# Four instructions of a 16-step turn moved by one step, and two PSUM banks exchanged

## The chip, the cores and the metric

One core of a Trainium2 chip. The metric is the device time of one execution in microseconds (us). A difference is worth telling from 0.2% on, which is 7 us here.

## What is computed

The input is normalised, `xn = (x - mean) / sqrt(var + 1e-5)`, for 16 sequences of 256 tokens with 128 channels. Two branches read it: a state-space branch `s` (short convolutions, a selective scan over 256 positions with 16 states) and a transformer of 6 layers, whose output goes through `silu` to give `g`. The result is `x + s * g`. The change lies in the transformer:

```python
def attn_layer(x, Wqkv, qs, ksc, Wo):
    q, k, v = jnp.split(x @ Wqkv, 3, -1)          # 16 heads of 64
    q = l2norm(q) * qs
    k = l2norm(k) * ksc
    q = q * cos * scale + rotate_half(q) * sin * scale
    k = k * cos * inv + rotate_half(k) * sin * inv
    out = local_attention(q, k, v)                # windows of 32, softmax
    return out @ Wo

def ffn_layer(x, g, bln, W1, b1, W2, b2):
    mu = x.mean(-1, keepdims=True)
    var = ((x - mu) ** 2).mean(-1, keepdims=True)
    xn = (x - mu) / jnp.sqrt(var + 1e-05) * g + bln
    a, gate = jnp.split(xn @ W1 + b1, 2, -1)
    return a * jax.nn.gelu(gate, approximate=False) @ W2 + b2

for i in range(6):
    x = attn_layer(shift_tokens(x), ...) + x
    x = ffn_layer(shift_tokens(x), ...) + x
```

## The kernel before

The tokens are cut into 8 groups of 512 (two sequences). The state-space branch comes first; its core time ends a little after 300 us. Then 6 layers of 8 groups, 48 items, pass through a software pipeline of **turns**. A turn has 16 **steps**, and works on up to four groups at a time: for `next` it makes the q and k blocks, for `cur` the attention, for `prev` the output projection and the feed-forward part up to its activations, for `prev2` the rest. A turn begins when the group before has moved on by one role. 46 turns have both a `prev` and a `next`.

Every engine has its own program of the same turns and steps, written out by hand, and takes its instructions strictly in the order of that program; semaphores tie the engines together. What an engine does in step s, as far as it is spoken of below:

- **TensorE (PE)**: the scores of pair and sequence s (`scores`, L847), then the first bank works of the step (L794 the transposes of q's norms, L892 the centring), the outputs of a pair in even steps (`outputs`, L875), the transposes of the probabilities (L856, L857), a block of v in odd steps, then the second bank works: the q or k block s of `next` (`project`, three matmuls of L360 to L362, called "block s" here), the three parts of the feed-forward gate (`g` 0, 1, 2 in steps 12, 13, 14) and of its other half (`a` 0 and 1 in step 14, `a` 2 in step 15), the variance (L896, step 8), and last the sums of squares (L829; four of them in a turn, one in step 8).
- **VectorE (DVE)**: reciprocals (`denominators`, L1635), copies of the transposed probabilities (L1641, L1642), the rotary products of block s-1 (`products`, L1610), the clamp of the sums (L1668, step 9), scaling of q's norms (`scale_q`, L1619 and L1620), `gated` (L1674, step 15), and last `maxima` (L1655, L1661), whose small result L1661 lets the scores of the next step start.
- **ScalarE (ACT)**: copies of outputs (L1193) or of v (L1198), the four exponentials of the probabilities (L1184), the norms of q and k (L1204 Ln, L1210 Exp) and of the layer norm (L1207 Ln, L1213 Exp), the squares of block s (`square`, L1172), the gelu of the gate (L1224, step 13, with a table load before and after it, L1224 and L1226), and xn_h, the high part of the normalised x (L1272, step 10).
- **GpSimd (POOL)**: scaling of the probabilities (`normalise`, L1345), the rotary sum of block s-2 (`rotate`, L1359), scaling of a key pair by its norms (`scale_k`, L1365), the layer norm's products (`normed`, L1375 and L1377, step 10), its low part (`low`, L1388, step 11), the low part of the next x (L1383, step 13).
- **SyncE (SP)** issues the DMAs: the swap of halves of each rotary product (L520), the spread of the key norms (L541), and others.

Ties between them that matter here:

```python
# DVE, products(j): the buffers ab and swp are two deep
dve.wait_ge(qk_rot, n16 + (16 * q + j - 1))     # rotate(j - 2) is done
# POOL, normed(prev), step 10
pool.wait_ge(f_rstd, ready)                     # ACT's L1213
# PE, outputs(s): v's copy of the step before
pe.wait_ge(v_sb, n8 + made)
# PE, scores(s), s even
pe.wait_ge(k_norm, scaled)                      # POOL's L1365 of this pair
```

The order of the bank works of PE, and the PSUM bank of each, is the table BANK_STEPS (L69 on). A work waits for the reader of the last work in its bank (`free_bank`): that is `square` for a block, gelu for `g`, `gated` for `a`, L1207 for `var`, `scale_q` for `rqT`. Blocks 11 to 15 all use bank 5. In step 14 `a` 0 uses bank 6, where `g` 1 was, and `a` 1 uses bank 4, where `g` 0 was. SCALE_STEPS (L117) gives POOL's steps of scale_k, AT (L77) the steps of most others. In five of the six layers two of the eight turns, "load" and "T0", also split the next layer's weights into high and low parts: ACT L1082 in steps 5, 9, 13 of "load" and 3, 5, 11 of "T0", POOL L1294 one step behind each.

Of the kernel before, what the change touches and what calls it, by code (L numbers as in the profile page):

```python
# [71 lines left out]
 [('next', 'qk', 8, 4), ('prev', 'cen', 0, 6), ('prev', 'var', 0, 6)], [('next', 'qk', 9, 5)],  # L72
 [('next', 'qk', 10, 4)], [('next', 'rqT', 0, 6), ('next', 'qk', 11, 5)],
 [('prev', 'g', 0, 4), ('next', 'qk', 12, 5)], [('prev', 'g', 1, 6), ('next', 'qk', 13, 5)],
 [('prev', 'g', 2, 7), ('next', 'qk', 14, 5), ('prev', 'a', 0, 6), ('next', 'sum', 1, 7), ('prev', 'a', 1, 4)],
 [('prev', 'a', 2, 6), ('next', 'qk', 15, 5)]]
NWO = 4  # L77
BACK = {"load": 10, "silu": {1: (0, 4), 3: (4, 7)}, "mul": 4, "halves": 3, "before": 2, "between": 4, "add": (8, 10, 11), "store": 12}
# [2 lines left out]
AT = {'wo': 2,  # L81
 'shift': 5,
 'residual': 6,
 'centred': 7,
 'ln_k': 8,
 'norm': 10,
 'high': 10,
 'low': 11,
 'gelu': 13,
# [1 line left out]
 'down': (16, 17, 19),  # L91
 'residual2': 19,
 'clamp': (9, 2),
 'scale_q': (11, 4),
 'k_out': (9, 2),
 'q_norm': 2,
 'next_shift': 8,
# [16 lines left out]
 14: ('next', 2),  # L114
 2: ('cur', 4),
 4: ('cur', 5)}
SCALE_STEPS = {13: [('cur', 7)],  # L117
 1: [('cur', 2)],
 7: [('cur', 5)],
 9: [('cur', 6)],  # L120
# [15 lines left out]
def build(nc, x_in, W_in, W_xdbl, W_dt, W_out, mvec, Wqkv, Wo, W1, W2, lvec, tabs_c, mask_c, ident_c,  # L136
          headsum_c, conv_w, out):
    ctx = ExitStack()
    with ctx:
# [154 lines left out]
        def use_bank(kind, i):  # L294

            return bank[BANK_OF[kind, i]]
# [28 lines left out]
        def group_of(role, o):  # L325

            return o[ROLES.index(role)]
# [669 lines left out]
        def _(act):  # L997
# [63 lines left out]
            def state_out(g):  # L1061

                after(act, m_s, g, 1, 1)
                after(act, m_sdma, g, 16, 0)
                act.activation(s_out, bank[2][:, :], ACT.Identity, bias=mv[:, M_BO:M_BO + 1]).then_inc(m_sout, 1)
# [9 lines left out]
            def split_high(layer, c):  # L1075

                total = 112 if c % 2 == 0 else 80
                due = {0: 32, 2: 64, 4: 96, 6: 112, 1: 32, 3: 48, 5: 64, 7: 80}[c]
                landed = total * layer + due
                act.wait_ge(raw_in[c % 2], landed)  # L1080
                src, hi, _ = chunk_views(c)
                act.activation(hi, src, ACT.Copy).then_inc(w_hi, 1)  # L1082
# [41 lines left out]
            def layer_tables(layer, part):  # L1124

                col = layer * NVEC + V_QS + part
                for i in (2 * part, 2 * part + 1):
                    ins = act.activation(ltab[:, i, :], tab[:, i, :], ACT.Identity, scale=lv_all[:, col:col + 1])
                ins.then_inc(tab_made, 1)
# [31 lines left out]
            def turn(n, o, par, gs, kind, l):  # L1161

                prev2, prev, cur, nxt = o
# [4 lines left out]
                def square(j, q):  # L1168
                    act.wait_ge(qk_mul, n16 + (16 * q + j + 1))
                    if j % 4 == 0 and (cur is not None or j >= 8):  # L1170
                        act.wait_ge(sq_part, n4 + (4 * q + j // 4 - 1))
                    act.activation(sq[:, j % NSQ, :], qk_bank(j, first)[:, :], ACT.Square).then_inc(qk_sq, 1)  # L1172

                def probabilities(s):

                    p, b = s // 2, s % 2
                    act.wait_ge(sc_bias, n16 + (s + 1))
                    if s >= 4 or prev is not None:
                        act.wait_ge(p_T, n16 + (s - 3))
                        act.wait_ge(p_Tsb, n16 + (s - 3))  # L1180
                    for i in range(2):
                        for t in range(2):
                            cs = slice(0, P) if t == 0 else slice(P, UW)
                            ins = act.activation(pr[:, s % 4, i, t, 0:P + WINDOW * t], sm[:, s % 2, i, cs], ACT.Exp,  # L1184
                                                 bias=nb[:, s, t, i:i + 1], scale=head_scale(rq, p, b)[:, t, i:i + 1],
                                                 accum_out=den[:, s, t, i:i + 1])
                    ins.then_inc(p_exp, 1)

                def copy_outputs(p, q):
                    act.wait_ge(o_ps, n8 + (8 * q + p + 1))  # L1190
                    if q == cur and prev is not None:
                        act.wait_ge(at_out, n4 + (4 * (q - 1) + p // 2 + 1))
                    act.activation(wide[:, p, :], bank[3][:, :], ACT.Copy).then_inc(o_sb, 1)  # L1193

                def copy_v(i, q):
                    c, tile = i // 4, i % 4
                    act.wait_ge(v_proj, n8 + (8 * q + i + 1))
                    act.activation(vtok[:, tile, c * VW:c * VW + VW], bank[3][:, :], ACT.Copy).then_inc(v_sb, 1)  # L1198

                def norms(h, q, ln):  # L1200

                    if q is not None:
                        act.wait_ge(sq_clamp, n2 + (2 * q + h + 1))
                        act.activation(rsum[:, :], rsum[:, :], ACT.Ln, scale=float(2 ** R_LOG2)).then_inc(r_ln, 1)  # L1204
                    if ln is not None:
                        act.wait_ge(f_var, n1 + (ln + 1))
                        act.activation(xv, use_bank("var", 0)[:, :], ACT.Ln, bias=eps[:, 0:1]).then_inc(f_ln, 1)  # L1207
                    if q is not None:
                        act.wait_ge(r_ln, n2 + (2 * q + h + 1))
                        act.activation(rsum[:, :], rsum[:, :], ACT.Exp, scale=-0.5).then_inc(r_exp, 1)  # L1210
                    if ln is not None:
                        act.wait_ge(f_ln, n1 + (ln + 1))
                        act.activation(xv, xv, ACT.Exp, scale=-0.5).then_inc(f_rstd, 1)  # L1213
# [20 lines left out]
                for s in range(16):  # L1234
                    if first and s == TAIL["out_sb"]:
                        state_out(GROUPS - 1)
                    if first and s in TAIL["split"]:
                        split_high(0, EARLY + TAIL["split"].index(s))
                    if s % 2 == 0 and s < 6 and prev is not None:
                        copy_outputs(s // 2 + 5, prev)  # L1240
                    if s % 2 == 0 and s >= 6 and cur is not None:
                        copy_outputs(s // 2 - 3, cur)
                    if s in V_STEPS and group_of(V_STEPS[s][0], o) is not None:
                        copy_v(V_STEPS[s][1], group_of(V_STEPS[s][0], o))
                    if s in SPLIT_AT.get(kind, ()):
                        split_high(nl, SPLIT_AT[kind][s])
                    if cur is not None:
                        probabilities(s)
                    if s == AT["q_norm"] and cur is not None:
                        norms(1, cur, None)  # L1250
                    if kind == "T2" and s == 1:
                        split_high(nl, 7)
                    if s == AT["centred"] and kind == "drain":
                        last_norm()
                    if s == AT["centred"] and prev is not None and kind != "drain":
                        act.wait_ge(f_cen, n1 + (prev + 1))
                        act.activation(xv, use_bank("cen", 0)[:, :], ACT.Square).then_inc(f_sq, 1)
                        act.activation(xn, use_bank("cen", 0)[:, :], ACT.Copy).then_inc(f_xc, 1)
                    if nxt is not None:
                        square(s, nxt)  # L1260
                        if kind == "load" and s >= 14:
                            layer_tables(nl, s - 14)
                    for role, _ in due("gelu", s):
                        if group_of(role, o) is not None:
                            gelu(group_of(role, o))
                    if s == AT["next_high"] and gs[2] is not None:
                        split_high_x(par)
                    if s == AT["ln_k"] and (nxt is not None or prev is not None) and kind != "drain":
                        norms(0, nxt, prev)
                    if s == AT["high"] and prev is not None and kind != "drain":  # L1270
                        act.wait_ge(f_gb, n1 + (prev + 1))
                        act.activation(xn_h[:, :], xn, ACT.Copy).then_inc(f_hi, 1)  # L1272
                    if kind == "drain" and s in BACK["silu"]:
                        silu(*BACK["silu"][s])
                        if s == max(BACK["silu"]):
                            act.preload_act_table_set("natural_log_exp_and_others")
# [8 lines left out]
        def _(pool):  # L1285
# [48 lines left out]
            def turn(n, o, par, gs, kind, l):  # L1334
# [55 lines left out]
                for s in range(16):  # L1390
# [12 lines left out]
                    if kind == "T2" and s in (1, 2):  # L1403
                        split_low(nl, 5 + s)
                    for role, p in SCALE_STEPS.get(s, ()):
                        if group_of(role, o) is not None:
# [409 lines left out]
```

## Time and profile before

| | us |
|---|---|
| three runs | 3594.86, 3596.83, 3598.45 (median 3596.83) |
| the profiled execution's own time | 3596.09 |
| its span, first to last instruction | 3594.3 |
| PE busy | 3394.7 (94%) |
| DVE busy | 3151.4 (88%) |
| ACT busy | 2999.4 (83%) |
| POOL busy | 2877.3 (80%) |
| granted TensorE clock, mean | 0.994 |

The profile is one execution. An engine's busy time is the union of its instructions; in a timeline, instructions of an engine can overlap by a tenth of a microsecond or so, so that the pitch from start to start is the cost of one in a queue, and start plus duration is when its result is there. Idle time is put down to whoever signalled last. In a pipeline of four nearly full engines the busy shares say little, and the waits within one turn say more.

### The profile page before, as it was taken

The numbers are of one execution on the slowest core, as the hardware profiler recorded it, in microseconds if no ns is written. First come the engines' busy times: TensorE is split into PE (matmuls) and PEld (weight loads), VectorE is DVE, ScalarE is ACT, GpSimd is POOL, SyncE is SP. The second block draws the span as 40 slices with busy tenths as digits, with TensorE's granted clock in tenths as the row PEclk, the third lists the DMA queues.
The fourth block names the chain that finished last, engine by engine and source line by source line (L and its number), as shares of the span: only waits on it lengthen the run. The fifth ranks groups of instructions, "written<-read, shape, count | busy, mean of one in ns | idle before, by whom it ended". The sixth has DMA issues, their size and how long they took to land.

```text
span 3594.3 us, 92498 instructions
## 1 busy us (share of the span) xinstructions
PE 3394.7 (94%) x29710; PEld 2110.8 (59%) x29710; DVE 3151.4 (88%) x10872; ACT 2999.4 (83%) x8812; POOL 2877.3 (80%) x2383
## 2 busy tenths in 40 slices
PE   7887999999999999999999999999999999999998
PEld 3444656656666666666656666666666656666665
DVE  7998988988988888988988988988988988988986
ACT  6554888888888888888888888888888888888887
POOL 6887887888887888887888887888887888887883
PEclk9998999999999999999999999999999999999999
DMA  5443322333323333322333322333332333332332
GB/s 164 141 133 124 113 99 102 108 115 108 115 101 101 106 112 106 116 103 99 107 115 107 116 102 99 110 116 103 115 106 96 108 118 105 114 106 99 106 103 92
DMA packets 261726, 396.22 MB, mean 110 GB/s; under 512 B 45566, under 2 KB 86588, under 8 KB 261244
## 3 DMA queue, kind: packets, MB, share of 16 engines
q1 hardware_dynamic: 261244, 390.30, 32.4%
q8 instruction: 240, 3.93, 0.5%
q14 instruction: 242, 1.98, 0.2%
HBM read 157.91 MB, written 6.03 MB: 46 GB/s over the span
## 4 chain that ended last, share of the span: by engine, by line
PE 53%; DVE 17%; POOL 14%; issue 7%; ACT 6%; DMA 2%; SPq 1%; DVEq 0%; POOLq 0%; ACTq 0%
PE bank L886 9%; PE bank L875 7%; PE bank L847 6%; PE bank L360 5%; PE bank L362 5%; PE bank L361 5%; DVE ab L1610 4%; PE bank L914 4%; PE bank L829 4%; POOL rot L1359 4%; POOL pr L1345 4%; PE bank L856 4%; DVE wide L1502 3%; PE bank L857 3%; DVE sm L1655 2%
## 5 line engine op out<-in xcount | busy, mean ns | idle before, releaser
L1184 ACT ACTIVATE pr<-sm,nb,rq 128x128 f32<-128x128 f32 (+1 forms) x3072 | 1518.0, 502 | 10.8 <-DVE nb L1661 10.7
L1345 POOL TENSOR_TENSOR pr<-pr,rden 128x640 f32<-128x640 f32 x768 | 966.2, 1258 | 460.1 <-DVE rden L1635 457.7
L1359 POOL TENSOR_TENSOR rot<-ab,swp 128x512 f32<-128x512 f32 x760 | 978.0, 1287 | 74.0 <-DMA swp<-ab 73.4
L1610 DVE TENSOR_TENSOR ab<-bank,ltab 128x1024 f32<-128x1024 f32 x760 | 925.1, 1217 | 80.6 <-PE bank L362 66.7
L1655 DVE CUSTOM_DVE_ANT_0 sm<-bank,mask 128x128 f32<-128x128 f32 (+1 forms) x3072 | 839.4, 328 | 47.5 <-PE bank L847 42.1
L1184 ACT ACTIVATION_READ_ACCUMULATOR pr<-sm,nb,rq 128x1 f32 x3072 | 599.5, 195 | 0.0
L847 PEld LDWEIGHTS bank<-rot 64*64 64x64 f32 x12288 | 288.1, 132 | 436.0 <-issue 364.7
L1365 POOL TENSOR_TENSOR rot<-rot,rkb 128x512 f32<-128x512 f32 x384 | 492.3, 1289 | 64.3 <-DMA rkb<-k_scratch 64.1
L1642 DVE COPY pt<-bank 128x512 f32<-128x512 f32 x768 | 531.3, 692 | 10.2
L875 PE MATMUL bank<-pt,vtok 128*64 128x160 f32 (+1 forms) x6144 | 461.6, 292 | 29.4 <-ACT vtok L1198 29.4
L1172 ACT ACTIVATE sq<-bank 128x512 f32<-128x512 f32 x768 | 452.6, 589 | 43.2 <-DVE ab L1610 19.9
L847 PE MATMUL bank<-rot 64*64 64x96 f32 x12288 | 431.9, 256 | 59.6 <-POOL rot L1365 34.9
L875 PEld LDWEIGHTS bank<-pt,vtok 128*64 128x64 f32 x6144 | 368.7, 136 | 202.1 <-issue 144.1
L1655 DVE DVE_READ_ACCUMULATOR2_ANT bank<- 128x1 f32 x3072 | 428.6, 140 | 0.0
L856 PE MATMUL bank<-ident,pr 128*128 128x128 f32 x1536 | 409.2, 293 | 10.7 <-DVE pt L1642 8.2
L1198 ACT ACTIVATE vtok<-bank 128x512 f32<-128x512 f32 x384 | 228.2, 594 | 225.3 <-PE bank L362 225.3
L857 PE MATMUL bank<-ident,pr 128*128 128x128 f32 x1536 | 377.7, 273 | 0.0
L886 PE MATMUL bank<-wide,wo 128*128 128x512 f32 x768 | 370.8, 605 | 0.0
L1193 ACT ACTIVATE wide<-bank 128x512 f32<-128x512 f32 x384 | 228.0, 594 | 160.9 <-PE bank L875 160.4
L360 PE MATMUL bank<-xh,wqk_h 128*128 128x512 f32 x768 | 339.6, 442 | 11.0 <-ACT sq L1172 7.6
L1641 DVE STREAM_TRANSPOSE pt<-pr 32x64 f32<-32x64 f32 x768 | 183.2, 239 | 173.3 <-PE bank L857 148.9
L362 PE MATMUL bank<-xl,wqk_h 128*128 128x512 f32 x768 | 305.4, 398 | 0.0
(213 smaller groups left out, 5743.7 us busy)
## 6 DMA issues: line engine op xcount, KB each, us to landing
swp<-ab SPq DMA_DIRECT2D x1520, 128.0 KB, 2.0
rkb<-k_scratch SPq DMA_DIRECT2D x768, 128.0 KB, 2.9
rot<-c_scratch SPq DMA_DIRECT2D x64, 256.0 KB, 3.3
sq<-c_scratch SPq DMA_DIRECT2D x64, 256.0 KB, 3.3
xs<-xT SPq DMA_DIRECT2D x95, 128.0 KB, 2.3
xs<-xT SPq DMA_DIRECT2D x95, 127.5 KB, 2.4
raw<-Wqkv SPq DMA_DIRECT2D x48, 128.0 KB, 2.7
wo<-Wo SPq DMA_DIRECT2D x6, 512.0 KB, 4.6
```

Of the source, the lines that this page charges most:

```text
L360: eng.matmul(o, wh, ah, start=True, stop=False)
L847: mm = pe.matmul(bank[i][part, c:c + 96], rot[rows, p, c0 + 64 * half:c0 + 64 * half + 64], rot[rows, PAIRS + p, c0 + k0:c0 + k0 + 96], st ...
L856: pe.transpose(bank[2][:, 256 * i:256 * i + P], pr[:, e % 4, i, 0, 0:P], ident[:, :])
L875: mm = pe.matmul(bank[3][64 * i:64 * i + 64, cols], vtok[:, 2 * b + t, ch], pt[:, e % 4, i, t, 0:cols.stop - cols.start], start=(b == 0 an ...
L886: mm = pe.matmul(use_bank("wo", 0)[:, :], wo[:, p, :], wide[:, p, :], start=(p == 0), stop=(p == PAIRS - 1))
L1184: ins = act.activation(pr[:, s % 4, i, t, 0:P + WINDOW * t], sm[:, s % 2, i, cs], ACT.Exp, bias=nb[:, s, t, i:i + 1], scale=head_scale(rq, ...
L1345: ins = pool.tensor_tensor(pr[:, e % 4, :, :, :], pr[:, e % 4, :, :, :], rden[:, e, :, :].rearrange("p t i -> p i t").unsqueeze(3) .to_bro ...
L1359: pool.tensor_tensor(rot[:, PAIRS * (j % 2) + j // 2, :], ab_of(j, 0, lead), swp_of(j, lead), ALU.add).then_inc(qk_rot, 1)
L1365: pool.tensor_tensor(rot[:, PAIRS + p, :], rot[:, PAIRS + p, :], rkb[:, p % KSLOT, :], ALU.mult)\
L1610: dve.tensor_tensor(ab_both(j, lead).rearrange("p i (b t) -> p i b t", b=GB), seqs(qk_bank(j, lead)[:, :]).unsqueeze(1).to_broadcast(shape ...
L1642: dve.tensor_copy(pt[:, e % 4, :, :, 0:P], bank[2][:, :].rearrange("p (i t c) -> p i t c", i=2, t=2)).then_inc(p_Tsb, 1)
L1655: ins = dve.tensor_tensor_reduce(sm[:, s % 2, i, cs], bank[i][:, cs], mask[:, cs], 1.0, -3e38, ALU.add, ALU.max, mx[:, t, i:i + 1])
```

## The change

- POOL: the scaling of key pair 7 of `cur` moves from step 13 to step 12.
- ACT: the layer norm's Ln and Exp (L1207, L1213) leave the function call of step 8, where they alternated with the Ln and Exp of q's and k's norms, and get a call of their own in step 9, after the squares of block 9.
- DVE: `scale_q(0)` of `next` (two instructions) moves from step 11 to step 12.
- PE: the banks of `a` 0 and `a` 1 are exchanged.

```diff
- [('prev', 'g', 2, 7), ('next', 'qk', 14, 5), ('prev', 'a', 0, 6), ('next', 'sum', 1, 7), ('prev', 'a', 1, 4)],
+ [('prev', 'g', 2, 7), ('next', 'qk', 14, 5), ('prev', 'a', 0, 4), ('next', 'sum', 1, 7), ('prev', 'a', 1, 6)],
...
  'ln_k': 8,
+ 'ln_n': 9,
...
- 'scale_q': (11, 4),
+ 'scale_q': (12, 4),
...
-SCALE_STEPS = {13: [('cur', 7)],
+SCALE_STEPS = {12: [('cur', 7)],
...
-                    if s == AT["ln_k"] and (nxt is not None or prev is not None) and kind != "drain":
-                        norms(0, nxt, prev)
+                    if s == AT["ln_k"] and nxt is not None and kind != "drain":
+                        norms(0, nxt, None)
+                    if s == AT["ln_n"] and prev is not None and kind != "drain":
+                        norms(0, None, prev)
```

In `norms(h, q, ln)` the Ln of q, the Ln of `ln`, the Exp of q and the Exp of `ln` stand in this order, each Exp waiting for its own Ln.

## Rows read from the trace of the kernel before

**Rows 1.** The page: busy time by engine

```profile
PE 3394.7 (94%) x29710; PEld 2110.8 (59%) x29710; DVE 3151.4 (88%) x10872; ACT 2999.4 (83%) x8812; POOL 2877.3 (80%) x2383
```

**Rows 2.** Chain of work that ended last, in one turn: start us, us, what

```profile
1513.19 1.04 PE bank L829 x8
...
1531.35 1.23 DVE ab L1610
1532.59 0.60 ACT sq L1172
...
1535.09 0.69 ACT gg L1224
1535.82 0.50 PE bank L360
```

**Rows 3.** Waits of PE, 1100 to 2100 us: total us, times, longest

```profile
PE bank L847 <- POOL rot L1365: 13.1, 15, 2.0
PE bank L875 <- ACT vtok L1198: 9.3, 15, 0.6
PE bank L360 <- ACT gg L1224: 7.5, 11, 1.0
PE bank L847 <- DVE nb L1661: 6.8, 15, 0.6
```

**Rows 4.** Timeline of PE: start us, us, what, [idle before it <- releaser]

```profile
432.63 1.20 PE L875 MATMUL bank<-pt,vtok 128*64 128x160 f32 x16 [0.62 <-ACT vtok L1198]
...
1517.76 1.20 PE L875 MATMUL bank<-pt,vtok 128*64 128x160 f32 x16 [0.62 <-ACT vtok L1198]
...
1540.80 0.44 PE L360 MATMUL bank<-xh,wqk_h 128*128 128x512 f32 x1
...
1585.14 1.20 PE L875 MATMUL bank<-pt,vtok 128*64 128x160 f32 x16 [0.62 <-ACT vtok L1198]
...
3479.45 1.20 PE L875 MATMUL bank<-pt,vtok 128*64 128x160 f32 x16 [0.62 <-ACT vtok L1198]
```

**Rows 5.** Timeline of ACT: steps 8 to 10 and 14, step 2 of the next turn

```profile
1514.98 0.63 ACT L1204 ACTIVATE rsum<-rsum 128x512 f32<-128x512 f32 x1 [0.34 <-DVE rsum L1668]
1515.51 0.67 ACT L1207 ACTIVATE gg<-bank,eps 128x512 f32<-128x512 f32 x1
...
1517.12 0.58 ACT L1198 ACTIVATE vtok<-bank 128x512 f32<-128x512 f32 x1
...
1520.05 0.58 ACT L1193 ACTIVATE wide<-bank 128x512 f32<-128x512 f32 x1
...
1522.97 0.63 ACT L1272 ACTIVATE xn_h<-gg 128x512 fp32r<-128x512 f32 x1
...
1540.12 0.58 ACT L1172 ACTIVATE sq<-bank 128x512 f32<-128x512 f32 x1
...
1556.08 0.61 ACT L1204 ACTIVATE rsum<-rsum 128x512 f32<-128x512 f32 x1
1556.72 0.63 ACT L1210 ACTIVATE rsum<-rsum 128x512 f32<-128x512 f32 x1
1557.26 0.58 ACT L1172 ACTIVATE sq<-bank 128x512 f32<-128x512 f32 x1
```

**Rows 6.** Timeline of POOL, steps 10 to 13 of the same turn

```profile
1518.83 1.29 POOL L1375 TENSOR_TENSOR gg<-gg 128x512 f32<-128x512 f32 x1
...
1523.67 1.28 POOL L1388 TENSOR_TENSOR xn_l<-gg,xn_h 128x512 fp32r<-128x512 f32 x1 [0.22 <-ACT xn_h L1272]
...
1528.59 1.31 POOL L1359 TENSOR_TENSOR rot<-ab,swp 128x512 f32<-128x512 f32 x1
1529.84 1.30 POOL L1365 TENSOR_TENSOR rot<-rot,rkb 128x512 f32<-128x512 f32 x1
```

**Rows 7.** Timelines of a later-running turn: POOL's L1359, then DVE's L1610

```profile
1113.91 1.29 POOL L1359 TENSOR_TENSOR rot<-ab,swp 128x512 f32<-128x512 f32 x1
...
1115.30 1.23 DVE L1610 TENSOR_TENSOR ab<-bank,ltab 128x1024 f32<-128x1024 f32 x1 [0.17 <-POOL rot L1359]
```

## The prediction

> **What bounds the kernel now.** I read the page's busy line first: PE is at 94% and every other engine at 80% or more [rows 1]. So at most some 6% lies in PE's waits, and the question is which of them sets the length of a turn. The timeline of PE gives that length: the outputs of step 10 wait in every turn in the same way, and from 1517.76 to 1585.14 us one turn takes 67.38 us [rows 4]. The first and the last of the 46 turns with this mark stand at 432.63 and 3479.45 us, so the mean of the 45 turns between is 67.71: a floor of 67.38, reached by about half, and some 15 us of excess in all (45 x 0.33), in turns in which POOL runs later.
>
> The chain of waits then says what holds the floor [rows 2]: PE up to the sums of squares of step 8 (end 1514.23), DVE from there without a gap to the products of block 13 (1531.35 to 1532.58), ACT's squares of block 13, the gelus, and PE's `a` 0 at 1535.82, just behind the second gelu's end (1535.09 + 0.69). From there to the next step 8 PE is full. One tie is hidden in this stretch: ACT's squares of block 14 end at 1540.12 + 0.58 = 1540.70 [rows 5], and PE's block 15, which needs that bank, starts at 1540.80 [rows 4]. PE has no more than 0.1 us there. So the turn's loop is: sums of step 8, clamp, DVE to products(13), ACT to square(14), PE from block 15 to the next sums.
>
> PE's four waits that the change touches [rows 3] are, per turn of these 15: 0.87 for the scaling of pair 7 at the scores of step 14, 0.62 for v's copy, 0.68 for the gelu (11 turns) and 0.45 for DVE's maxima. All lie between 1514 and 1536, where PE waits for the others anyway.
>
> **The change part by part, in the turn of 1517.**
>
> *Scaling of pair 7, POOL.* It goes before the scaling of probabilities and rotate(11) of step 13. It costs nothing itself, and the scores' wait goes. But rotate(11) comes later by its pitch, 1529.84 - 1528.59 = 1.25 us. Products(13) needs rotate(11); it ended at 1528.59 + 1.31 = 1529.90 against 1531.35 [rows 6, 2]: of 1.45 us of slack 0.2 is left. No DMA is moved; SP's spread of the next pair's norms, which waits for this scaling, and the swap behind it can only go sooner.
>
> *Layer norm's Ln and Exp, ACT.* They were hidden in step 8. Now the first pair runs alone: Exp follows its Ln after 0.64 and the next instruction after 0.54 more [rows 5] (the pair of step 2), so v's copy starts at 1514.98 + 1.18 = 1516.16 instead of 1517.12, ends at 1516.74, before PE's outputs want it (1517.14, the mark less 0.62), and the 0.62 us wait goes. From v's copy over the probabilities and squares of step 9 to the copy of step 10 it was 1520.05 - 1517.12 = 2.93 us [rows 5]; so the layer norm's Ln starts at 1516.16 + 2.93 = 1519.09. With Ln 0.67 and some 0.03 of handing over, Exp runs from 1519.79 to 1520.41, and with 0.07 of handing over to POOL (1522.97 + 0.63 to 1523.67 [rows 5, 6]) `normed` can start at 1520.48. It started at 1518.83, with no wait for the Exp of step 8 [rows 6]. **POOL now waits 1.65 us in step 10.** Behind that wait on POOL's queue are rotate(9), (10) and (11), and DVE waits for each.
>
> On the overlap of ScalarE instructions, the rows show what splitting costs [rows 5]: the four took 2.14 us, the two pairs take 1.18 + 1.21 = 2.39, that is 0.25 more. The Trainium skill (ScalarE: Activation LUTs, section What ACT_TABLE_LOAD costs) puts the overlap of two ACTIVATEs back to back at about 93 ns; two overlaps lost would be 0.19, an estimate from that page, and the sum would be 0.06 us a turn smaller.
>
> *The chain on POOL.* From normed's start to rotate(11)'s end the old queue took 1529.90 - 1518.83 = 11.07, of which 0.22 was a wait for xn_h [rows 6]. That wait goes (xn_h is up at 1523.9, low starts at 1525.1), and pair 7 comes in: 11.07 - 0.22 + 1.25 = 12.10. So rotate(11) ends at 1520.48 + 12.10 = 1532.58, and DVE takes 0.10 to start behind it (1113.91 + 1.29 to 1115.30 [rows 7]): products(13) at 1532.68 against 1531.35, **1.33 us late**. Rotate(9) holds DVE up before that, so no slack is left on its side; rows 7 show DVE waiting for POOL in just this way in a turn where POOL ran late.
>
> *Banks of `a`, PE.* `a` 0 now waits for the first gelu, 0.6 us earlier. With 1.33 of delay in front, `a` 0 starts about 0.7 later than before instead of 1.33. But block 15 waits for ACT's square(14), which moves by the full 1.33; the 0.6 us is lost there, since PE had at most 0.1 to spare. I take 0. Bounds: a gain of 0.1 (the tie) and, if square(14) were not last, 0.6.
>
> *scale_q, DVE.* Two instructions, 0.19 us, go from before nb(11) to before nb(12). The sum up to products(13) is the same: 0. Nobody needs them before the next turn, and the bank they free is wanted by `g` 1 in step 13. Bounds: nothing to a gain of 0.19.
>
> *The layer norm's bank* is freed by Ln at 1519.76; the transposes of q's norms want it about 1520.6. Nothing, with 0.8 us of cover.
>
> **Sum.** A plain turn becomes 67.38 + 1.33 = 68.71. Turns that ran late before had POOL late already; they come to the same 68.71, since POOL's start is now set by ACT. In 5 "load" turns ACT's split of step 9 stands before Ln, 0.5 more: 69.2. In 5 "T0" turns POOL's split of step 12 stands before rotate(11), one POOL pass of 1.25: 69.95. That is 36 x 68.71 + 5 x 69.2 + 5 x 69.95 = 3169.3, against 3046.8 + 67.4 = 3114.2 for the 46 turns now: **+55 us**. The profiled execution took 3596.09, 0.7 under the median; so 3651 against a median of 3597, +1.5%.
>
> **Bounds for a turn.** Low: POOL's wait 1.65 passes on only in part, if the 0.2 and 0.1 of slack, 0.19 of scale_q and 0.25 of splitting all help: about 0.6 less, 0.7 a turn, +27 us. High: the whole 1.65 in every turn on top of today's mean, 46 x 1.65 = +76 us.
>
> **A rule against this sum.** POOL's passes lasted 1.28 to 1.31 whether DVE stood or ran [rows 6, 7]. The Trainium skill (GPSIMD Engine Reference, section Specifications) has GpSimd's SBUF interfaces shared with VectorE, in contention when that engine has two SBUF inputs. By it POOL would run faster while DVE waits and win part of the delay back. With the shortest duration in these rows for the longest, 9 passes give 9 x 0.03 = 0.3 us, and the turn 68.4: within my range, and the rows speak against it.
>
> **The rivals.**
> 1. *Faster: the cover holds.* If products(13) does not wait for rotate(11), since DVE or PE is later than I think, POOL's lateness stays hidden, and what remains are the gains: the scores' wait, which makes the late turns, goes (15 us), and the tie gives 0.1 in 46 turns (5 us). Time 3577. It decides at a lateness of POOL under 0.2 us at rotate(11), the slack left; for it speaks only that PE loses four waits; against it 1.65 us.
> 2. *No change:* the delay is paid from slack in the second half of the turn (the table loads, POOL's idle time in the next steps 0 to 5) and the bank exchange gives its 0.6. With 0.3 of old excess gone and 0.4 won back behind the gelus, 1.33 - 0.6 - 0.3 - 0.4 leaves nothing: 3597 to 3605. Against it: PE has no wait from 1540.80 on, so nothing can be caught up.
> 3. *Slower still:* later products mean later swaps on SP's queue, and rotate waits for their DMA as it does in some turns now: another 0.4 us a turn, 3670.
>
> **How the numbers follow.** My forecast, a turn longer by 0.9 to 1.5, has 0.72; rival 1 0.10, rival 2 0.11 (half of it within 0.2%), rival 3 0.07. The predicted time is 3651. The range goes from 3608, which takes in the low bound and a part of rival 2, to 3675, the high bound and rival 3. A measurement here can tell 0.2%, 7 us, from no change. Faster 0.10, within 0.2% 0.06, slower 0.84.
>
> **What would show it.** In the changed profile: no wait of PE for L1198 at the outputs of step 10; L1375 with some 1.6 us of idle time before it, released by ACT's L1213; DVE's L1610 waiting for POOL's L1359 in nearly all turns (now 0.17 in late ones); `a` 0 waiting less for L1224; PE's L360 of block 15 waiting about 0.7 for L1172; the turn 68.7. I am wrong if L1375 starts without a wait, if L1610 does not wait for L1359, or if turns stay under 67.5.

## The result, and the profile after

| | before | changed |
|---|---|---|
| median of 4 runs each, us | 3597.64 | 3655.65 |
| lowest and highest, us | 3594.86, 3600.67 | 3654.21, 3656.35 |
| profiled execution's own time, us | 3596.09 | 3656.20 |
| its span, us | 3594.3 | 3654.4 |

The changed kernel takes 1.0162 of the time before (95% interval 1.0147 to 1.0177): +58 us. The forecast was 3651, with 3608 to 3675 as its range. All medians and ratios here are of runs in the chip's usual, fast state; one of the four runs of "norm move alone" fell in the slow one (5475.63 us) and is left out.

The loss is spread evenly. Between the 46 marks of a turn (ACT's L1204 behind its wait for DVE, L1205 in the changed kernel), the 45 turns took 3046.8 us before and 3104.4 after. The commonest turn went from 67.38 to 68.73, and no turn is shorter than that by more than 0.03. The excess over that floor, 15 us before, is now 12 us, nearly all of it in the ten "load" and "T0" turns.

The page's busy line of the changed kernel answers to the one of before [rows 1]:

```profile
PE 3405.6 (93%) x29710; PEld 2107.7 (58%) x29710; DVE 3159.3 (86%) x10872; ACT 3020.2 (83%) x8812; POOL 2876.4 (79%) x2383
```

The number of instructions is the same on each engine, and POOL has the same busy time (2877.3 before). ACT's busy time is 20.8 us longer, though the durations of its instructions sum to 21.5 us less (3781.7, before 3803.2): they overlap less. No engine got more work; the 58 us are waits and lost overlap.

The chain of waits of the changed kernel in one turn, start us, us, what, against [rows 2]:

```profile
1532.44 1.04 PE bank L830 x8
1533.50 0.70 DVE rsum L1671
1534.22 0.64 ACT rsum L1205
1535.43 0.58 ACT vtok L1199
1536.01 1.96 ACT pr L1185 x8
1537.97 0.48 ACT sq L1173
1538.45 0.58 ACT gg L1208
1539.05 0.64 ACT gg L1214
1539.85 1.28 POOL gg L1378
...
1548.10 1.30 POOL rot L1368
1549.40 1.21 POOL pr L1348
1550.61 1.25 POOL rot L1362
1551.95 1.24 DVE ab L1613
1553.21 0.60 ACT sq L1173
...
1560.83 0.49 ACT sq L1173
1561.36 0.50 PE bank L361
```

Before, the chain went from the sums of step 8 through DVE. Now it goes clamp, ACT to the layer norm's Exp (L1214), POOL's `normed` (L1378), POOL's queue with pair 7 (L1368) in it, rotate(11) (L1362 at 1550.61 here, 1550.55 in the timeline), products(13) (L1613 at 1551.95), and then as before over the gelus and the squares of block 14 to PE's block 15.

The waits themselves, in the timelines of ACT, POOL, DVE and PE in this turn:

```profile
1538.35 0.68 ACT L1208 ACTIVATE gg<-bank,eps 128x512 f32<-128x512 f32 x1
1539.05 0.63 ACT L1214 ACTIVATE gg<-gg 128x512 f32<-128x512 f32 x1
1539.59 0.58 ACT L1194 ACTIVATE wide<-bank 128x512 f32<-128x512 f32 x1
...
1543.03 0.59 ACT L1199 ACTIVATE vtok<-bank 128x512 f32<-128x512 f32 x1
...
1536.84 1.28 POOL L1362 TENSOR_TENSOR rot<-ab,swp 128x512 f32<-128x512 f32 x1
1539.85 1.28 POOL L1378 TENSOR_TENSOR gg<-gg 128x512 f32<-128x512 f32 x1 [1.74 <-ACT gg L1214]
...
1543.19 1.29 POOL L1362 TENSOR_TENSOR rot<-ab,swp 128x512 f32<-128x512 f32 x1
...
1546.86 1.29 POOL L1362 TENSOR_TENSOR rot<-ab,swp 128x512 f32<-128x512 f32 x1
...
1550.55 1.30 POOL L1362 TENSOR_TENSOR rot<-ab,swp 128x512 f32<-128x512 f32 x1
...
1544.58 1.23 DVE L1613 TENSOR_TENSOR ab<-bank,ltab 128x1024 f32<-128x1024 f32 x1 [1.13 <-POOL rot L1362]
1548.26 1.23 DVE L1613 TENSOR_TENSOR ab<-bank,ltab 128x1024 f32<-128x1024 f32 x1
1551.95 1.23 DVE L1613 TENSOR_TENSOR ab<-bank,ltab 128x1024 f32<-128x1024 f32 x1
...
1555.86 0.50 PE L361 MATMUL bank<-xn_h,w_h 128*128 128x512 f32 x1 [1.03 <-ACT gg L1225]
...
1561.36 0.50 PE L361 MATMUL bank<-xh,wqk_h 128*128 128x512 f32 x1 [0.38 <-ACT sq L1173]
```

POOL waits 1.74 us in step 10, in this turn. Over the 46 turns this wait is anything from none to 1.74 us, because POOL arrives more or less late; but `normed` starts 5.60 us behind L1205 in most of them, since ACT sets its start. DVE waits 1.13 at products(11) for rotate(9). At products(12) and (13) the profile lists no wait, but they are 3.68 us apart, and 3.46 us before: each starts 0.1 behind the end of a rotate (1550.55 + 1.30 = 1551.85, then 1551.95). From L1205 to products(13) it is 17.73 us, before 1531.35 - 1514.98 = 16.37 [rows 2, 5]: 1.36 us more, the turn's 1.35.

The waits of PE in 1100 to 2100 us of the changed kernel, total us, times, longest, against [rows 3]:

```profile
PE bank L361 <- ACT gg L1225: 14.5, 14, 1.0
PE bank L876 <- ACT vtok L1199: 9.6, 15, 1.1
PE bank L848 <- DVE nb L1664: 7.5, 28, 0.4
PE bank L361 <- ACT sq L1173: 6.9, 15, 1.0
PE bank L857 <- DVE pt L1645: 6.7, 14, 0.5
PE bank L361 <- POOL xn_l L1391: 5.6, 15, 0.4
```

The wait for pair 7, 13.1 us before, is gone. The wait for v's copy has only moved, from step 10 to step 12: v's copy of step 11 starts at 1543.03, 8.81 us behind L1205, where it was 8.51 before. The 0.30 us are the price of splitting the pairs on ACT (below); ACT has no other wait up to there.

### The profile page after: what moved, and what is told of

It is laid out like the page before. It is cut to its first block, busy times and chain, and to the rows that moved or that the text cites. A ratio compares the mean times of both kernels' runs of the same rounds, so it can differ in the third digit from the quotient of the medians.

```text
span 3654.4 us, 92498 instructions
## 1 busy us (share of the span) xinstructions
PE 3405.6 (93%) x29710; PEld 2107.7 (58%) x29710; DVE 3159.3 (86%) x10872; ACT 3020.2 (83%) x8812; POOL 2876.4 (79%) x2383
## 4 chain that ended last, share of the span: by engine, by line
PE 53%; POOL 14%; DVE 13%; ACT 11%; issue 7%; DMA 0%; DVEq 0%; SPq 0%; POOLq 0%; ACTq 0%
PE bank L887 9%; PE bank L876 7%; PE bank L848 6%; POOL pr L1348 5%; PE bank L361 5%; PE bank L363 4%; PE bank L362 4%; DVE ab L1613 4%; PE bank L915 4%; PE bank L830 4%; PE bank L857 4%; POOL rot L1362 3%; DVE wide L1505 3%; ACT pr L1185 3%; PE bank L858 2%
## 5 line engine op out<-in xcount | busy, mean ns | idle before, releaser
L1613 DVE TENSOR_TENSOR ab<-bank,ltab 128x1024 f32<-128x1024 f32 x760 | 926.3, 1219 | 133.0 <-POOL rot L1362 62.9
L1362 POOL TENSOR_TENSOR rot<-ab,swp 128x512 f32<-128x512 f32 x760 | 974.9, 1283 | 74.7 <-DMA swp<-ab 74.2
L1185 ACT ACTIVATION_READ_ACCUMULATOR pr<-sm,nb,rq 128x1 f32 x3072 | 590.0, 192 | 0.0
L1368 POOL TENSOR_TENSOR rot<-rot,rkb 128x512 f32<-128x512 f32 x384 | 492.1, 1288 | 65.8 <-DMA rkb<-k_scratch 65.2
L857 PEld LDWEIGHTS bank<-ident,pr 128*128 128x128 f32 x1536 | 214.6, 140 | 161.4 <-issue 142.8
```

Of the source, the lines that this page charges most:

```text
L857: pe.transpose(bank[2][:, 256 * i:256 * i + P], pr[:, e % 4, i, 0, 0:P], ident[:, :])
L1362: pool.tensor_tensor(rot[:, PAIRS * (j % 2) + j // 2, :], ab_of(j, 0, lead), swp_of(j, lead), ALU.add).then_inc(qk_rot, 1)
L1368: pool.tensor_tensor(rot[:, PAIRS + p, :], rot[:, PAIRS + p, :], rkb[:, p % KSLOT, :], ALU.mult)\
L1613: dve.tensor_tensor(ab_both(j, lead).rearrange("p i (b t) -> p i b t", b=GB), seqs(qk_bank(j, lead)[:, :]).unsqueeze(1).to_broadcast(shape ...
```

## The experiments

The change touches five instructions in all: one of POOL, two of ACT and two of DVE. Each was compared with the kernel before on the same chip. "Floor" is the commonest length of a turn in its profile.

| run | floor, us | ratio to before (95%) | median, us |
|---|---|---|---|
| before | 67.38 | | 3597.6 to 3599.3 |
| the change | 68.73 | 1.0162 (1.0147 to 1.0177) | 3655.65 |
| norm move alone | 68.48 | 1.0131 (1.0114 to 1.0148) | 3644.52 |
| all but the norm move | 67.39 | 1.0024 (1.0014 to 1.0034) | 3605.65 |
| pair 7 alone | 67.39 | 1.0030 (1.0019 to 1.0041) | 3608.68 |
| banks alone | 67.39 | 0.9998 (0.9989 to 1.0008) | 3597.32 |
| scale_q alone | 67.40 | 0.9997 (0.9988 to 1.0007) | 3599.38 |
| norm before the probabilities | 67.70 | 1.0047 (1.0032 to 1.0062) | 3613.80 |
| norm before the squares | 68.26 | 1.0097 (1.0082 to 1.0112) | 3635.14 |
| banks, squares of block 14 first | 66.77 | 0.9938 (0.9922 to 0.9955) | 3575.70 |
| squares of block 14 first alone | 67.35 | 0.9997 (0.9988 to 1.0007) | 3597.98 |
| the change, squares first | 68.10 | 1.0086 (1.0071 to 1.0101) | 3631.36 |
| probabilities last in step 13 | 67.40 | 1.0004 (0.9995 to 1.0014) | 3598.45 |
| banks, squares first, probabilities last | 66.77 | 0.9947 (0.9932 to 0.9962) | 3577.94 |

### The change taken apart

**The norm move alone**, on the kernel before:

```diff
-                        norms(0, nxt, prev)
+                        norms(0, nxt, None)
+                    if s == AT["ln_n"] and prev is not None and kind != "drain":
+                        norms(0, None, prev)
```

> Only the layer norm's Ln and Exp are moved to step 9; pair 7 stays in step 13, scale_q in step 11, the banks as before. My theory (POOL waits for the Exp in step 10, and DVE's products wait for POOL's rotate behind it): POOL's L1375 waits 1.65 us, rotate(10) ends 1.9 us later than before and products(13) 1.07 us later, so a plain turn takes 68.4 to 68.5 and the kernel +38 to +45 us, about 3638. Rival A (most of the loss is pair 7 in front of rotate(11)): under +20 us. Rival B (ACT's own 0.25 us of splitting the pairs is the loss): +12 us.

+47 us, 2 above the 38 to 45 expected; the floor is 68.48, in the 68.4 to 68.5 expected. POOL waits 17.9 us in 14 turns for the Exp, and DVE for rotate. In 1100 to 2100 us, DVE's waits for rotate in this run:

```profile
DVE ab L1613 <- POOL rot L1362: 15.5, 18, 1.2
```

and in the kernel before:

```profile
DVE ab L1610 <- POOL rot L1359: 2.7, 7, 0.9
```

So this part carries four fifths of the loss, and rivals A and B fall.

**All but the norm move**: the changed kernel with `norms(0, nxt, prev)` back in step 8.

> Everything of the change but the layer norm's move. My theory: no wait in front of POOL's normed, so turns in which POOL is on time take 67.3 to 67.4; turns in which POOL runs late lose more than now, since pair 7 stands before rotate(11): 0 to +20 us, about 3605. Rival A (pair 7's move is the loss): +35 us or more. If the four waits of PE were worth anything by themselves it would be faster than before by 15 to 25 us.

+0.24%, or 8 us, with the floor back at 67.39. PE's wait for pair 7 is gone, the one for the gelu has grown from 7.5 to 13.7 us, and nothing is gained.

**Pair 7 alone**:

```diff
-SCALE_STEPS = {13: [('cur', 7)],
+SCALE_STEPS = {12: [('cur', 7)],
```

> Only the scaling of pair 7 moves from step 13 to step 12. My theory: its price of 1.25 us on POOL is covered by 1.45 us of slack in a turn on time, and not in a late one: the same as the run without the norm's move within 5 us, so 0 to +20 us. PE's wait at the scores of step 14 goes. Rival A: +35 us or more. A gain of 10 us or more would show that PE's wait for pair 7 was what made the late turns.

+0.30%, or 11 us, floor 67.39: covered in a turn on time, lost in late ones, whose excess over the floor is 27 us in this profile and 15 before. PE's waits in 1100 to 2100 us:

```profile
PE bank L360 <- ACT gg L1224: 22.0, 15, 1.6
PE bank L875 <- ACT vtok L1198: 9.3, 15, 0.6
PE bank L847 <- DVE nb L1661: 6.8, 15, 0.6
```

The 13.1 us for pair 7 are gone, and the wait for the gelu at `a` 0 has gone from 7.5 to 22.0 us: PE is there sooner and waits there instead. This is what it means that the wait was not on the path.

**Banks alone**:

```diff
-('prev', 'a', 0, 6), ('next', 'sum', 1, 7), ('prev', 'a', 1, 4)
+('prev', 'a', 0, 4), ('next', 'sum', 1, 7), ('prev', 'a', 1, 6)
```

> Only the banks of a 0 and a 1 exchanged. My theory: PE's wait for the gelu at a 0 falls from about 0.7 to 0.1 to 0.4 us, and the same time comes back as a wait of block 15 for ACT's squares of block 14 (tied within 0.1 us before): 0 to -5 us. Rival (the gelu wait is on the path by itself): 0.6 us x 46 = -27 us.

No change. The two waits in this run's profile, 1100 to 2100 us:

```profile
PE bank L360 <- ACT sq L1172: 4.7, 12, 0.5
...
PE bank L360 <- ACT gg L1224: 1.7, 5, 0.4
```

The gelu wait fell from 7.5 to 1.7 us, and the wait for the squares rose from 1.0 to 4.7.

**scale_q alone** (`'scale_q': (12, 4)`):

> The kernel before with only scale_q moved from step 11 to step 12. My theory: PE's wait for DVE's maxima at the scores of step 12 falls by 0.19 us a turn, and the time stays within 3 us, since DVE's own queue up to products(13) is as long as before. Rival (that wait is on the path): -9 us.

No change, though PE's wait for the maxima fell from 6.8 to 3.9 us in the same stretch, by 0.19 a turn. Again PE only met the next wait earlier: the one for v's copy rose from 9.3 to 11.8.

### The dose of POOL's wait

In two runs of the changed kernel the layer norm's pair stands earlier in step 9.

**Before the squares of block 9** (0.48 us earlier):

```diff
                     if cur is not None:
                         probabilities(s)
+                    if s == AT["ln_n"] and prev is not None and kind != "drain":
+                        norms(0, None, prev)
```

> The changed kernel with the layer norm's Ln and Exp in front of the squares of block 9 instead of behind them: 0.48 us earlier. A dose of the suspected wait. My theory: POOL's wait falls by 0.48 and each turn on time with it, 68.73 to 68.25, so 46 x 0.48 = 22 us less than the changed kernel, about 3633. Rival (a threshold: it matters only that the Exp stands behind the exponentials of step 9): as the changed kernel, 3655.

The floor is 68.26, where 68.25 was expected, the time 3635.14 (20 us under the changed kernel, 22 if each is taken against the kernel before on its own chip), and POOL's wait in one of its turns 1.25 instead of 1.74:

```profile
1532.09 1.28 POOL L1378 TENSOR_TENSOR gg<-gg 128x512 f32<-128x512 f32 x1 [1.25 <-ACT gg L1214]
```

0.48 us on ACT is 0.47 us a turn: no threshold lies between these two places.

**Before the probabilities of step 9** (the same two lines in front of `if cur is not None`):

> The changed kernel with one thing different: the layer norm's Ln and Exp stand in step 9 right behind v's copy, in front of the probabilities, some 2.4 us earlier on ACT, and everything else of the change stays, the splitting into two pairs with its 0.25 us too. My theory (the whole loss is POOL's wait for the Exp, with pair 7's 1.25 us on top): the Exp ends at about 1517.9 on the scale of the profiled turn, before POOL wants it (1518.8), the wait is gone, and the time is that of the run without the norm's move, 3600 to 3610. Rival (splitting and the later probabilities are the loss): it stays at 3640 or more.

The floor is 67.70 and the time 3613.8, 4 us above the range given. POOL's wait is gone (L1378 in the first row), which settles the main cause:

```profile
1523.86 1.29 POOL L1378 TENSOR_TENSOR gg<-gg 128x512 f32<-128x512 f32 x1
```

but something of the rival is true as well. The 0.31 us above 67.39 is a wait of DVE for the exponentials of step 9:

```profile
1521.16 0.17 DVE L1638 RECIPROCAL rden<-den 128x4 f32<-128x4 f32 x1
1525.03 0.18 DVE L1638 RECIPROCAL rden<-den 128x4 f32<-128x4 f32 x1 [0.32 <-ACT pr L1185]
```

Here the four activations stand in front of the probabilities as before, only in two pairs. The pairs take 0.31 us longer: in the changed kernel 1534.22 to 1535.43 and, from the layer norm's Ln to the next copy, 1538.35 to 1539.59, together 1.21 + 1.24 = 2.45, against 2.14 [rows 5]. In this place the exponentials that DVE waits for stand behind both pairs.

### The tie at block 15

**Banks and the squares of block 14 first**, on the kernel before:

```diff
+                    if s == 14 and nxt is not None:
+                        square(s, nxt)
                     if cur is not None:
                         probabilities(s)
...
                     if nxt is not None:
-                        square(s, nxt)
+                        if s != 14:
+                            square(s, nxt)
```

> The kernel before with the banks exchanged and, in step 14, ACT's squares of block 14 in front of the four exponentials, so 2 us earlier. My theory (the bank exchange alone gives nothing because block 15 waits for these squares): both together give most of 0.6 us a turn where POOL is on time, -12 to -27 us, about 3577. Rival (PE's block 15 was not tied to the squares): no gain over the banks alone. A loss is possible if the exponentials, 0.5 us later, hold DVE's reciprocals of the next step.

0.9938, 22 us less than before, floor 66.77, which is 0.61 less: about the time from one gelu to the next, which is what `a` 0 gains by the banks. DVE does wait for the later exponentials now, which costs nothing here:

```profile
DVE rden L1638 <- ACT pr L1184: 12.7, 16, 0.9
```

**The squares first alone:**

> The kernel before with ACT's squares of block 14 in front of the exponentials of step 14, banks as before. My theory (two waits lie one behind the other on PE, a 0 for the second gelu and block 15 for the squares, within 0.1 us of each other): each cure alone gives at most that 0.1, so -0 to -6 us, floor of a turn 67.3 to 67.4, where both gave 66.77. Rival (the squares alone were the bound, and the banks did nothing in the run with both): -20 us.

No change, floor 67.35. Each half gives 0.0 to 0.03 us a turn, both together 0.61: PE's two waits lay one behind the other.

**The changed kernel with the squares first:**

> The changed kernel with ACT's squares of block 14 in front of the exponentials of step 14. In the changed kernel block 15 waits 0.37 us for these squares, and a 0 has gained from the banks what is lost there. My theory: a turn on time gets 0.37 shorter, 68.36, so -17 us against the changed kernel, about 3638. Rival (POOL's rotate(12) and block 14's products set the pace too): no gain.

3631.36, 24 us under the changed kernel, floor 68.10: 0.63 less, not the 0.37 expected. I had taken the 0.37 from the row of PE's wait for the squares, and the rest was not in that row. Block 15 behind the last matmul of `a` 2, in the changed kernel and then before:

```profile
1560.60 0.39 PE L363 MATMUL bank<-xn_l,w_h 128*85 128x512 f32 x1
1561.36 0.50 PE L361 MATMUL bank<-xh,wqk_h 128*128 128x512 f32 x1 [0.38 <-ACT sq L1173]
1561.70 0.39 PE L362 MATMUL bank<-xh,wqk_l 128*128 128x512 f32 x1
```

```profile
1540.57 0.39 PE L362 MATMUL bank<-xn_l,w_h 128*85 128x512 f32 x1
1540.80 0.44 PE L360 MATMUL bank<-xh,wqk_h 128*128 128x512 f32 x1
1541.08 0.39 PE L361 MATMUL bank<-xh,wqk_l 128*128 128x512 f32 x1
```

The row counts idle time from the end of the matmul before. Without a wait, block 15 starts 0.16 us before that end (1540.80 against 1540.57 + 0.39 = 1540.96), and its second matmul follows after 0.28 instead of 0.34. So the wait costs 0.38 + 0.16 + 0.06 = 0.60 of the 0.63; for the last 0.03 no row accounts. The run with the banks alone shows the same: `a` 0 starts 0.58 sooner behind L1204 than before and block 15 only 0.05 sooner, with 0.38 listed. The rival falls.

### The late turns

**The scaling of the probabilities last in POOL's step 13**, on the kernel before, so that rotate(11) and pair 7 come 1.2 us sooner:

```diff
-                    if s >= 2 and cur is not None:
+                    if s >= 2 and s != 13 and cur is not None:
                         normalise(s - 2, cur)
...
+                    if s == 13 and cur is not None:
+                        normalise(s - 2, cur)
                     if s == AT["next_low"] and gs[2] is not None:
```

> The kernel before, but in POOL's step 13 rotate(11) and the scaling of pair 7 stand in front of the scaling of the probabilities, which nobody needs for 1.7 us: both 1.2 us earlier. My theory (what makes turns longer than 67.4 us is POOL late for rotate(11) and pair 7): the excess of 15 us goes in good part, -5 to -15 us, about 3587, with PE's wait for pair 7 near 0. Rival (the excess comes from elsewhere): within 3 us.

A miss: no change, as the rival had it. PE's wait for pair 7 did fall, from 13.1 to 2.2 us, but its wait for the gelu rose from 7.5 to 16.9. The waits of POOL and DVE in 1100 to 2100 us of this run:

```profile
POOL rot L1359 <- DMA swp<-ab: 33.5, 41, 2.0
```

```profile
DVE ab L1612 <- POOL rot L1359: 17.9, 21, 1.7
```

Rotate waits more for its swap's DMA (33.5 us, before 24.1), and DVE more for rotate (17.9, before 2.7).

**All three on the kernel before** (banks, squares first, probabilities last):

> The kernel before with the banks exchanged, ACT's squares first in step 14, and the scaling of the probabilities last in POOL's step 13. If the two effects add, -20 to -40 us, about 3567; if one bound hides the other, the better of the two single runs.

0.9947, no better than the two without the third.

## Why the prediction was right

- *What bounds a turn.* The loop from the sums of step 8 over DVE and ACT to PE's block 15 holds. Three of the four waits of PE are worth nothing when removed or shortened alone (pair 7, banks, scale_q) or together (all but the norm move); the fourth, for v's copy, goes only with the splitting of ACT's pairs and was not tested alone. And moving ACT's squares pays only where the theory said.
- *POOL's wait of 1.65 us.* It is 1.74 by its row, and 1.78 as the sum counted it, from start to start (1539.85 - 1534.22 = 5.63, before 1518.83 - 1514.98 = 3.85). The Exp ends 5.46 us behind L1205, where the sum had 5.43; the term that was small is the handing over to POOL, 1539.05 + 0.63 = 1539.68 to 1539.85, so 0.17 us instead of the 0.07 that was read from another pair of instructions. In the other turns it is 0.14 to 0.17.
- *The splitting of the pairs.* It costs 0.3 instead of 0.25 us. The Trainium skill (ScalarE: Activation LUTs, section What ACT_TABLE_LOAD costs) has back-to-back ACTIVATEs overlap by about 93 ns, and the rows agree (1514.98 + 0.63 = 1515.61 against 1515.51 [rows 5], 0.10). Two lost overlaps, 0.19 by that page, are an estimate that comes out too low: the dependent Exp also starts 0.03 behind the end of its Ln, twice, which is half of the 0.11 missing.
- *The chain behind it.* Products(13) comes 1.36 us late, I had 1.33, and the plain turn is 68.73, I had 68.71. That the two agree so well is in part luck: the 0.1 us missing in the handing over is made up by POOL's queue from `normed` to rotate(11), which took 1551.85 - 1539.85 = 12.00 us instead of 12.10. One link was told loosely: without pair 7 the floor is still 68.48, since rotate(9) and rotate(10) hold DVE up first. Products(13) starts 17.49 us behind L1205 there, with no wait for rotate(11), against 17.73; so pair 7 adds only 0.24 of its 1.25 us.
- *The low bound.* Its four terms sum to 0.74 us, not to about 0.6, which leaves 0.59 a turn and the +27 us given, not 0.7; and the 0.25 of splitting is a cost inside the sum and no slack. The 3651 does not use it; the lower end of the range does, and the measured time is far from there.
- *Load and T0 turns.* 69.25 to 69.58 for the five behind a "load" step 9, as said (69.2). The T0 turns took 69.98 to 70.90, mean 70.35, not 69.95: the term was 0.4 too small, 2 us in all. In each of them PE also waits 1.0 us for the squares of block 13 before block 14, which I had not followed.
- *Sum.* +55 forecast, +58 measured: 45 turns give 57.6. The T0 term is 2 of the 3 us.
- *Banks: nothing.* Right, and shown on the kernel before: -0.02% alone. The expected signs were in part right. `a` 0 starts 1555.86 - 1534.22 = 21.64 us behind L1205, before 20.84, so 0.80 later, where 0.7 was said. Block 15 starts 1561.36 - 1534.22 = 27.14 behind it, before 25.82, so 1.32 later, as the sum had it. But `a` 0 does not wait less for the gelu (1.03, before 0.96 in the same turn); and block 15's listed wait is 0.38, not 0.7, though its cost is 0.60, as told under the tie.
- *Rule of the shared interface.* POOL's rotate(9) took 1.29 us while DVE stood from 1543.45 to 1544.58, and 1.28 to 1.31 before [rows 6, 7]: POOL did not speed up, and nothing of the delay was won back that way. The prediction put the page to the wrong use. The Trainium skill (GPSIMD Engine Reference, section Specifications) names VectorE instructions in a 2-port perf mode or with two SBUF inputs, and DVE's products read one input, `bank`, from PSUM and only `ltab` from SBUF. By the second condition no contention was to be expected, and the trace agrees; whether an instruction here runs in a 2-port mode it does not show. All 768 passes of L1362 in the changed kernel took 1.26 to 1.32 us, and the eight beside which DVE stood idle throughout 1.26 to 1.30.
- *Rival 1, faster,* falls with POOL's wait; its price for the late turns was wrong too, since taking pair 7's wait away made those turns longer, not shorter (pair 7 alone, +11 us). *Rival 2* counted on 0.6 us of the banks that did not come by themselves; the 0.6 is real, and comes once the squares are out of the way. *Rival 3*, later swaps, did not show: POOL's waits for the swaps did not grow (20.4 us in 1100 to 2100 us, 24.1 before).

What stays open is what makes turns late when POOL has no wait for the norm. The excess over the floor differs from one profile to the next, the order in POOL's step 13 does not cure it, and the DMA of the swaps is suspected only because rotate waits for it.

## What to carry to other kernels

Before moving an instruction to a later place on one engine, look at who takes its result and how full that engine is behind it: here an Exp that came 3.2 us later on ACT used up 1.6 us of unseen slack on POOL and made a turn 1.35 us longer (1.28 in the mean of 45 turns). The longest waits of the busiest engine need not be worth anything: removing one may only bring the engine to its next wait sooner. So follow the loop to where that engine stops waiting, and look for a second wait hidden there within a tenth of a microsecond. Two such waits must be cured together: here either alone gave 0, both gave 0.6%.

## What was not expected of the hardware

- Two dependent activations back to back cost more than four interleaved: Exp started 0.67 us (L1211) and 0.70 (L1214) behind its Ln, where the activation behind an Ln before followed after 0.54 and 0.57, and the four took 2.45 instead of 2.14 us.
- The time that a wait of PE costs is larger than its row: 0.38 us was listed for the squares, and 0.63 us came back when they were moved out of the way. Of the difference, 0.16 us is the overlap with the matmul before, which a waiting matmul loses, and 0.06 a slower start of the block.
- Handing a result from ACT to POOL took 0.07 us for xn_h [rows 5, 6] and 0.14 to 0.17 for the layer norm's Exp.
